# Turning the convolved input by DMA instead of on TensorE in a Mamba block: step sizes folded into exponents, eight places fewer in the bank ring, input norms split

## The reference

```python
x = input @ Wx.T; z = input @ Wz.T               # 512 wide
x = silu(causal_conv(x, conv_w, conv_b))         # 4 taps over time
b = x @ Wb.T; c = x @ Wc.T                       # 8 heads x 64 states
dt = softplus(x @ Wdt.T + b_dt)                  # one step size per token and head
# scan over time, per head:
state = exp(dt_t * a) * state + (dt_t * b_t) x_t ;  y_t = c_t . state
y = y + d_param * x                              # then norm per head, gate with silu(z), @ Wout.T
```

## Time and profile before

| | us |
|---|---|
| median of 3 runs | 1266.62 (1266.29 to 1266.91) |
| the profiled execution | 1265.6 |
| its span, first to last instruction | 1263.9 |
| PE busy in it | 1218.3 (96%) |
| DVE busy | 997.3 (79%) |
| ACT busy | 878.6 (70%) |
| POOL busy | 465.5 (37%) |

### The profile page before, as it was taken

How to read it: one execution, slowest core, us unless ns; L and a number is a source line. 1 busy time by engine, 2 the same in 40 slices (tenths; PEclk the granted TensorE clock), 3 DMA queues, 4 the chain that set the end, 5 groups by cost and what they waited for, 6 DMA issues and landing times.

```text
span 1263.9 us, 27616 instructions
## 1 busy us (share of the span) xinstructions
PE 1218.3 (96%) x10306; PEld 765.1 (61%) x10306; DVE 997.3 (79%) x2385; ACT 878.6 (70%) x1554; POOL 465.5 (37%) x557
## 2 busy tenths in 40 slices
PE   7999999999999999999999999999999999999896
PEld 5665657565565756656566565756656575564674
DVE  6666877788787796978779787778878789787687
ACT  6675677667776687766966678667787668776365
POOL 2131236142451524416343243623336152441332
PEclk9999999999999999999999999999999999999999
DMA  8011101111020110202111020111112111020001
GB/s 239 1 35 36 34 17 35 43 42 36 18 68 17 35 34 18 68 18 53 26 41 35 18 68 18 35 38 26 55 17 52 34 18 34 18 68 17 2 1 51
DMA packets 91829, 48.09 MB, mean 38 GB/s; under 512 B 63120, under 2 KB 89892, under 8 KB 91696
## 3 DMA queue, kind: packets, MB, share of 16 engines
q1 hardware_dynamic: 91696, 46.33, 14.9%
HBM read 22.72 MB, written 8.39 MB: 25 GB/s over the span
## 4 chain that ended last, share of the span: by engine, by line
PE 76%; DVE 14%; issue 5%; ACT 2%; POOL 2%; DVEq 0%; ACTq 0%; POOLq 0%
PE bank L1728 34%; PE bank L1945 8%; PE bank L1928 8%; PE bank L1837 5%; PE bank L1815 4%; PE bank L1899 3%; DVE xs L1303 3%; PE bank L1905 3%; PE bank L1873 3%; PE bank L1807 2%; PE bank L1860 2%; PE bank L1851 2%; DVE gn_stats L1442 2%; DVE yT L1481 1%; PE bank L1826 1%
## 5 line engine op out<-in xcount | busy, mean ns | idle before, releaser
L937 POOL TENSOR_TENSOR Cd<-Cd,CT 128x512 f32<-128x512 f32 x64 | 93.8, 1465 | 359.8 <-ACT Cd L1180 359.4
L1728 PE MATMUL bank<-sh,WbT 128*128 128x512 f16 x768 | 171.5, 379 | 1.9 <-DVE sh L1308 1.2
L1728 PE MATMUL bank<-sh,WcT 128*128 128x512 f16 x768 | 171.3, 379 | 0.0
L1208 ACT ACTIVATE hf<-bank,vectors,alpha 128x512 f32<-128x512 f32 x128 | 99.0, 776 | 52.0 <-PE bank L1928 30.2
L1303 DVE SCALAR_TENSOR_TENSOR xs<-xi,vectors,xs 128x512 f32<-128x512 f32 x168 | 125.1, 749 | 9.4 <-ACT xs L1085 5.7
L1728 PEld LDWEIGHTS bank<-sh,WcT 128*128 128x128 f16 x768 | 75.2, 98 | 86.6
L1728 PEld LDWEIGHTS bank<-sh,WbT 128*128 128x128 f16 x768 | 72.9, 98 | 87.1 <-DVE sh L1308 6.1
L1928 PE MATMUL bank<-uh,sign1T 128*128 128x512 f16 x512 | 121.6, 380 | 1.8 <-issue 1.7
L1945 PE MATMUL bank<-sign2T,hh 128*128 128x256 f16 x1024 | 117.2, 273 | 1.2 <-DVE hh L1543 1.1
L1945 PEld LDWEIGHTS bank<-sign2T,hh 128*128 128x128 f16 x1024 | 97.8, 98 | 21.7 <-ACT hf L1208 6.5
L868 POOL TENSOR_TENSOR rstd_mid<-var_eps_mid,power 128x4 f32<-128x4 f32 x16 | 16.2, 1011 | 227.3 <-DVE var_eps_mid L1258 227.3
(11 more groups left out here) (235 smaller groups left out, 2600.1 us busy)
## 6 DMA issues: line engine op xcount, KB each, us to landing
xt<-L_attn_input_tensor_dram SPq DMA_DIRECT2D x17, 512.0 KB, 4.1
u<-L_attn_input_tensor_dram SPq DMA_DIRECT2D x15, 512.0 KB, 3.9
out_dram<-u SPq DMA_DIRECT2D x15, 512.0 KB, 3.0
yT<-in_L_ffn_w_dram SPq DMA_DIRECT2D x2, 512.0 KB, 8.8
u<-in_L_ffn_w_dram SPq DMA_DIRECT2D x2, 512.0 KB, 9.3
BT<-in_L_attn_Wx_dram SPq DMA_DIRECT2D x1, 512.0 KB, 5.1
BT<-in_L_attn_Wz_dram SPq DMA_DIRECT2D x1, 512.0 KB, 4.5
zs<-in_L_attn_Wb_dram SPq DMA_DIRECT2D x1, 512.0 KB, 6.2
```

Of the source, the lines that this page charges most:

```text
L937: pool.tensor_tensor(Cd[n % 2][:, :, :], Cd[n % 2][:, :, :], CT[:, :, q * P:(q + 1) * P], ALU.mult)\
L1208: nc.scalar.activation(hf[f % 2][:, :], bank(t, ("H", j, f))[:, :], ACT.Gelu, bias=b1_col[:, f:f + 1], scale=alpha1[:, f:f + 1]).then_inc( ...
L1728: mm = nc.tensor.matmul(bank(t, key)[:, :], w[i][:, k, cols(m)], v[h][:, k, :], start=(a == 0), stop=(a == len(terms) - 1))
```

## The change

X leaves PE. SP issues, per chunk, two DMA transposes, one of each fp16 part of the convolved input, from `sh_rows`, whose layout is now tokens in runs of 128 per chunk (`[P, NQ, KI, P]`), into `x_turned`, which lies in chunks 3 and 0 of the tile `xi` (two buffers, for odd and even chunks). DVE adds the two parts into `xdt`, which now is 256 times the input, without the step size. The step size goes into the exponents: DVE floors it (`dt_floor`), ACT takes the logarithm of a 256th of it (`log_dt`), DVE spreads its negative over a wide tile (`log_wide`), and PE adds it with one more product each into `cums` and `sums`. The projections write and read through a view by chunk.

The bank ring has no X, so 107 places per element. The step `in_norm` is split: the high passes (`in_high`) stay in place, the four full passes come after `front` 2, and `xT` moves from before `front` 2 to between `carry` 1 and `back` 1; `end_tiles` moves behind `back` 1. In a first block ACT's `fold` of the tail comes before `gelu_table`, and `gelu_table` follows the new `ln_dt`. Some small tiles share memory (`abs_v` with `exp_v`, `e_rest` with `e_back`, `dt_floor` with `dt_raw`, `log_dt` with `log_u`), with waits for it.

```diff
@@ -192,10 +193,10 @@
-        steps += own(("log", j))
-        steps += tail(("mid_norm", j)) + own(("B", j, 1), ("decay", j)) + tail(("gelu_table",))
+        steps += own(("X", j, 0), ("X", j, 1), ("log", j))
+        steps += tail(("mid_norm", j)) + own(("B", j, 1), ("decay", j)) + tail(*[("fold", 1, m) for m in range(2 if j == 0 else 0)])
...
-        steps += tail(*[("fold", 1, m) for m in range(2 if j == 0 else 0)], ("ff_stat", j))
+        steps += own(("ln_dt", j)) + tail(("gelu_table",), ("ff_stat", j)) + own(("ln_wide", j))
@@ -218,20 +219,20 @@
 
-        norm, xT = [(who, "in_norm", nj)], [(who, "xT", nj), (who, "load", nj)]
+        norm, xT = [(who, "in_high", nj)], [(who, "xT", nj), (who, "load", nj)]
         steps += own(("decays", j), ("ends", j, 0), ("front", j, 0)) + ([(who, "in_mean", nj)] if first else []) + out[0]
...
             steps += weights(("alpha2", 0))
-        steps += own(("score", j, 1), ("carry", j, 0)) + norm + (own(("head_stat", 0, 0)) if j else [])
-        steps += out[1] + own(("back", j, 0)) + xT
+        steps += own(("X", j, 2), ("score", j, 1), ("X", j, 3), ("carry", j, 0)) + norm + (own(("head_stat", 0, 0)) if j else [])
+        steps += out[1] + own(("back", j, 0))
         def end(*keys):
...
 
-        steps += own(("E", j, 2), ("ends", j, 2), ("seg", j, 2), ("front", j, 2), ("score", j, 2)) + end(("end_tiles", j))
-        steps += own(("carry", j, 1), ("back", j, 1), ("E", j, 3), ("ends", j, 3), ("seg", j, 3), ("front", j, 3))
+        steps += own(("E", j, 2), ("ends", j, 2), ("seg", j, 2), ("front", j, 2)) + [(who, "in_norm", nj)]
+        steps += own(("score", j, 2), ("carry", j, 1)) + xT + own(("back", j, 1)) + end(("end_tiles", j)) + own(("E", j, 3), ("ends", j, 3), ("seg", j, 3), ("front", j, 3))
         steps += end(("end_mean", j)) + (end(("end_root", j)) if j else []) + own(("score", j, 3))
@@ -330,10 +331,12 @@
+        x_turned = [xi[:, KI - 1 if r else 0, 0:BLK].bitcast(F16).rearrange("p (i c f) -> p i c f", i=2, c=KI) for r in range(2)]
...
-        sh = [sb(f"sh{i}", [P, KI, BLK], F16) for i in range(2)]
+        sh_rows = [sb(f"sh{i}", [P, NQ, KI, P], F16) for i in range(2)]
+        sh = [v[:, :, :, :].rearrange("p q c t -> p c q t") for v in sh_rows]
@@ -342,12 +345,14 @@
-        v_dt, abs_v, exp_v, one_e, e_back, e_rest, log_u = (small(n) for n in (
-            "v_dt", "abs_v", "exp_v", "one_e", "e_back", "e_rest", "log_u"))
+        v_dt, exp_v, one_e, e_back, log_u = (small(n) for n in ("v_dt", "exp_v", "one_e", "e_back", "log_u"))
+        abs_v, e_rest = exp_v, e_back
...
+        dt_floor, log_dt = dt_raw, log_u
+        log_wide = sb("log_wide", [P, HP, PARTS, NQ * KI])
@@ -424,7 +429,7 @@
-                return [*[("seg", *at, g) for g in range(HP)], ("X", *at), ("Bt", *at)]
+                return [*[("seg", *at, g) for g in range(HP)], ("Bt", *at)]
@@ -511,6 +516,10 @@
+        x_rows = [Signal(sem(f"x_rows{r}"), NCH // 2, step=32) for r in range(2)]
+        ln_in = Signal(sem("ln_in"), NJ)
+        ln_out = Signal(sem("ln_out"), NJ)
+        ln_wide = Signal(sem("ln_wide"), NJ * HP)
@@ -810,6 +825,18 @@
+            def turn_tokens(t, j, q):
+                n = ch(j, q)
+                r = q % 2
+                s, sj, sq = two_before(t, n)
+                if q == 0:
+                    sp.wait_ge(*conv_out.count(t, (j + 1) * KI * (TAPS - 1)))
+                    sp.wait_ge(*sh_hi.count(t, (j + 1) * KI))
+                    sp.wait_ge(*sh_lo.count(t, (j + 1) * KI))
+                sp.wait_ge(*xdt_out.count(s, ch(sj, sq) + 1))
+                for i in range(2):
+                    sp.dma_start_transpose(x_turned[r][:, i, :, :], sh_rows[i][:, q, :, :].rearrange("p c t -> p (c t)")).then_inc(x_rows[r].sem, 16)
@@ -1022,14 +1050,16 @@
-            def input_norm(t, j):
-                if opening(t) and j == 0:
-                    return
+            def input_high(t, j):
...
+            def input_norm(t, j):
+                if opening(t) and j == 0:
+                    return
@@ -1056,7 +1086,6 @@
-                act.wait_ge(*full(s, ("X", sj, NQ - 1)))
@@ -1066,6 +1095,7 @@
+                    act.wait_ge(*xdt_out.count(s, (sj + 1) * NQ))
@@ -1117,15 +1147,24 @@
-                nc.scalar.activation(sh[0][:, c, :], xs[:, c, :], ACT.Copy, scale=SX).then_inc(sh_hi.sem, 1)
+                    for landed in x_rows:
+                        act.wait_ge(*landed.count(s, (sj + 1) * NQ // 2))
+                nc.scalar.activation(sh[0][:, c], by_chunk(xs[:, c, :]), ACT.Copy, scale=SX).then_inc(sh_hi.sem, 1)
...
+                p, pj = before_block(t, j)
+                act.wait_ge(*full(p, ("sums", pj)))
+                act.wait_ge(*ln_wide.count(p, (pj + 1) * HP))
...
+            def step_size_log(t, j):
+                act.wait_ge(*ln_in.count(t, j + 1))
+                nc.scalar.activation(log_dt[:, :, :], dt_floor[:, :, :], ACT.Ln, scale=1.0 / SX).then_inc(ln_out.sem, 1)
@@ -1337,7 +1380,9 @@
+                p, pj = before_block(t, j)
...
+                dve.wait_ge(*ln_out.count(p, pj + 1))
@@ -1348,14 +1393,25 @@
-                p, pj = before_block(t, j)
...
+                nc.vector.tensor_scalar(dt_floor[:, :, :], dt_t[:, :, :], DT_FLOOR, None, ALU.max).then_inc(ln_in.sem, 1)
...
+            def step_wide(t, j):
+                p, pj = before_block(t, j)
+                dve.wait_ge(*full(p, ("cums", pj)))
+                dve.wait_ge(*ln_out.count(t, j + 1))
+                raw = log_dt[:, :, :].rearrange("p q h -> p (q h)")
+                for g in range(HP):
+                    v = of_side(raw, g)[:, None].to_broadcast([P, PARTS // 2, NQ * KI // 2, 2])
+                    nc.vector.tensor_scalar(log_wide[:, g, PARTS // 2:PARTS, :].rearrange("p m (n f) -> p m n f", f=2), v, -1.0, None,
+                                            ALU.mult).then_inc(ln_wide.sem, 1)
@@ -1404,11 +1460,11 @@
-                for need in latest(full(t, ("X", j, q)), full(s, ("Y", sj, sq, HP - 1))):
-                    dve.wait_ge(*need)
+                dve.wait_ge(*full(s, ("Y", sj, sq, HP - 1)))
...
-                nc.vector.tensor_tensor(xdt[r][:, :, :], heads(bank(t, ("X", j, q))[:, :]), per_head(dt_t[:, q, :]),
-                                        ALU.mult).then_inc(xdt_out.sem, 1)
+                dve.wait_ge(*x_rows[q % 2].count(t, n // 2 + 1))
+                hi, lo = [x_turned[q % 2][:, i, :, :].rearrange("p c f -> p (c f)") for i in range(2)]
+                nc.vector.tensor_tensor(xdt[r][:, :, :], heads(hi), heads(lo), ALU.add).then_inc(xdt_out.sem, 1)
@@ -1725,7 +1781,7 @@
-                    mm = nc.tensor.matmul(bank(t, key)[:, :], w[i][:, k, cols(m)], v[h][:, k, :], start=(a == 0),
+                    mm = nc.tensor.matmul(by_chunk(bank(t, key)[:, :]), w[i][:, k, cols(m)], v[h][:, k], start=(a == 0),
@@ -1782,13 +1838,19 @@
-                                 start=True, stop=True).then_inc(full_sem(t, key), 1)
+                                 start=True, stop=False)
+                pe.wait_ge(*ln_wide.count(t, (j + 1) * HP))
+                nc.tensor.matmul(bank(t, key)[:, 0:P], log_wide[:, :, :, :].rearrange("p g a n -> p (g a n)"), ident[:, :],
+                                 start=False, stop=True).then_inc(full_sem(t, key), 1)
...
-                nc.tensor.matmul(bank(t, key)[:, 0:NQ * HEADS], after[:, :], da[:, :], start=True, stop=True)
+                nc.tensor.matmul(bank(t, key)[:, 0:NQ * HEADS], after[:, :], da[:, :], start=True, stop=False)
+                pe.wait_ge(*ln_out.count(t, j + 1))
+                nc.tensor.matmul(bank(t, key)[:, 0:NQ * HEADS], ident[:, :], log_dt[:, :, :].rearrange("p q h -> p (q h)"),
+                                 start=False, stop=True)
@@ -1807,13 +1869,12 @@
-                for name, src in (("X", xs), ("Bt", BT)):
-                    key = (name, j, q)
-                    for need in latest(empty(t, key), B_out.count(t, (j + 1) * KI), C_out.count(t, (j + 1) * KI)):
-                        pe.wait_ge(*need)
-                    for c in range(KI):
-                        mm = nc.tensor.transpose(bank(t, key)[:, cols(c)], src[:, c, cols(q)], ident[:, :])
-                    mm.then_inc(full_sem(t, key), 1)
+                key = ("Bt", j, q)
+                for need in latest(empty(t, key), B_out.count(t, (j + 1) * KI), C_out.count(t, (j + 1) * KI)):
+                    pe.wait_ge(*need)
+                for c in range(KI):
+                    mm = nc.tensor.transpose(bank(t, key)[:, cols(c)], BT[:, c, cols(q)], ident[:, :])
+                mm.then_inc(full_sem(t, key), 1)
```

35 lines of the change are left out of this document (22 added, 13 removed).

## The result

The changed kernel takes 1278.55 us (median of 4 runs, 1277.94 to 1279.25) where the kernel before takes 1266.57 (4 runs beside it): ratio 1.0095, 95% interval 1.0077 to 1.0112. It is 12.0 us slower. The forecast was 5.9 slower: the sign was right and 1278.55 lies in the wide range of 1254 to 1284, just above the 1269 to 1278 given to the forecast itself, but only half of the loss was foreseen. The profiled execution took 1277.94, its span is 1276.2.

A forecast was written before the change was run, and what follows sets the result against it. PE works 96% of the span, but waits on DVE and the DMA were taken to limit the gain. 5.6 + 4.2 - 3.5 + 2.1 - 2.5 = +5.9 on 1265.6 gives 1271.5, as median 1272.5 us; range 1254 to 1284.

The forecast's parts named there:

- the sign: Whole kernel: the change was forecast to make it slower, by 5.9 us, with a 60% chance given to slower.
- Added products: PE, every block: two more products for the exponents, 0.46 us a block, +5.6 us in all (bounds 3.6 and 9.9).
- the wait of H for uT: PE in block A, an element's second half: an idle of 0.22 us before H hides added products in 8 blocks.
- Block B: First half of the next element: DVE's state comes sooner, so the next block starts 0.5 us earlier, x7: -3.5.
- The string under the waits in A: Second half of an element: xT starts near 582.9, xi at 587.3, so 0.2 us is gained of 2.1.
- The waits themselves: PE in block A: stalls of 1.1 us before B's turn of chunk 3 and 1.2 us before xi.
- the contention of `xdt` with GpSimd: DVE's xdt reads two SBUF tensors beside GpSimd work: 0.15 us per chunk stage, 14 times, +2.1 (bounds 0 and 0.5 each).
- the landing: DMA of xT's low half in block A: taken to land 3.1 us after xT ends, at 587.3.
- The ring: Element border: with 107 places xi(0,1) waits for DVE's back of chunk 3, +0.6 us at 7 borders, +4.2.
- First and last block: Blocks with no tail or no next: X off PE saves some of its time, -2.5 us in all (bounds 0, -4).
- The deeper premise: PE, 64 chunks: X's transposes take some 0.5 us each chunk, so 31 us is the most that can be won.
- Rival 1: PE is the bound all along and the waits are not met: -31 + 5.6, 1241 us; 6% chance.

The follow-up runs named there:

- experiment 12: Changed kernel with xdt made from the high half of the turned X alone, one SBUF input instead of two: 1272.29 us, ratio 1.0048 to the kernel before.
- experiment 2: Changed kernel with three empty places in the bank ring, 110 per element: 1271.86 us, ratio 1.0050 to the kernel before.
- experiment 8: Changed kernel with three empty ring places and the next element's first xi product one step later, behind chunk 2's carried work: 1263.89 us, ratio 0.9981 to the kernel before.
- experiments 1: Changed kernel with xT and the input norms back in their old places, X still off PE: 1275.33 us, ratio 1.0070 to the kernel before.
- experiment 3: Changed kernel with xT and the norms in their old places and three empty ring places: 1271.11 us, ratio 1.0039 to the kernel before.
- Experiment 5: Kernel before with one of the four transposes of each X turn on PE, the other three left out: 1258.29 us, ratio 0.9938 to the kernel before.
- experiment 7: Kernel before with only the move of norms, xT and end sums, X still on PE: 1284.34 us, ratio 1.0136 to the kernel before.

## Why the prediction had the sign right and only half the size

- **Added products: right, with some luck.** 5.6 was forecast for 16 blocks; 5.5 is measured in 15 and 0.45 in the first. Thirteen of the 16 cost 0.40 to 0.45, three A blocks 0.04 to 0.16. So the wait of H for uT hides them in three A blocks, not in eight, and there it hides more than the 0.22.
- **Block B: right in mechanism and size.** YI of chunk 3 was put at 667.05 and stands at 667.04; -0.5 each was forecast, -0.6 measured. DVE's string is the one that was counted forward: 0.72 of waiting for GpSimd's state (0.6 forecast), and the state of chunk 3 at 666.5 in the frame (666.6). The agreement to 0.01 is chance.
- **The string under the waits in A: the step that failed.** The waits themselves were named rightly, 1.1 and 1.2 forecast, 1.08 and 1.09 measured, but the string that sets them was priced too low in two terms. The first is the contention of `xdt` with GpSimd, taken at 0.15 a chunk stage "as most of it falls in waits". In A it doesn't: it goes through `Cd`, `xdw` and `state` on GpSimd into `carry` 1, `xT` and the transfer, and is worth 0.5 or more (experiment 12). `xT` was put at 582.9 and stands at 583.5, xi at 587.3 and is at 587.9. In B it does fall in waits, as far as that run shows. The rule of the Trainium skill that the prediction cites (GPSIMD Engine Reference, the specifications table) agrees with these rows, but the sum needed a price. The second term is the landing, taken at 3.1 after the issue: two of seven took 4.3 and 4.4 (see the landings below).
- **The ring: right in mechanism, 0.6 forecast, 0.8 measured** per border (experiment 2), 1.3 us more in all. Together with the contention this is more than the 2.4 by which the typical A blocks miss; what gave the rest back I didn't trace.
- **Not in the sum at all: landings that vary.** A typical A costs 1.1, 0.35 over the 0.75 that the ring and the contention gave it, 2.4 in seven. Three of seven cost 2.2 to 2.4 and make another 3.6. In two of them the low half lands 4.3 and 4.4 us after its issue instead of 3.1; PE's rows:

```profile
898.64 1.46 PE L1784 MATMUL bank<-xh,WxT 128*128 128x512 f16 x6 [2.32 <-issue]
...
1051.98 1.46 PE L1784 MATMUL bank<-xh,WxT 128*128 128x512 f16 x6 [2.35 <-issue]
```

  In the third, block 1, a stretch at a lower granted clock (0.60) follows waits of 0.27 and 1.25; the columns of the windows are as above:

```profile
127.45 0.65 PE L1876 MATMUL bank<-ident,BT 128*128 128x128 f32 x4 [1.25 <-DVE yT L1491]
128.03 1.37 PE L1898 MATMUL bank<-CT,BT 64*128 64x128 f32 x16
129.33 1.12 PE L1912 MATMUL bank<-xdw,bt 128*64 128x64 f32 x16
...
130.00:132.80 2.80, 2.80 (x42) 2.22 (x38) 1.17 (x4) 0.70 (x2) 0.61 (x1) 0.60 0.00 0
```

  Experiment 2 has the same waits there (0.28 and 1.24), keeps its full clock, and its block 1 costs no more than a typical one, so the third block's price is the clock's. The 5.0 at the end of the earlier trace rows was there to be read. The kernel before had 1.2 to 3.0 us between the landing and xi, the changed one has none, so the median of the landings was the wrong figure for a sum. The 2.4 and the 3.6 are A's miss of 6.0 (11.2 measured, 5.25 forecast), and A's miss is about the forecast's.
- **First and last block:** -2.5 forecast, -0.2 in the changed kernel's profiled execution (with 0.45 of added products in it). Most of the miss is the clock in the last block. There PE waits 2.97 us for `Cd` in all kernels of this order, and what its clock does then differs. Windows of 15 us that begin just before that wait, of the changed kernel, experiment 2 and experiment 8 (columns as above), have a granted clock of 0.77, 0.89 and 1.00, and the stretch from the last `seg` of chunk 0 to the end is 0.3, 1.6 and 3.0 shorter than before:

```profile
1180.00:1195.00 15.00, 10.99 (x104) 7.90 (x103) 9.16 (x20) 8.80 (x15) 6.75 (x6) 0.77 0.19 36
```

```profile
1175.00:1190.00 15.00, 10.98 (x119) 7.72 (x119) 10.11 (x21) 9.40 (x16) 7.18 (x7) 0.89 0.20 37
```

```profile
1167.00:1182.00 15.00, 10.87 (x148) 7.69 (x150) 11.76 (x23) 9.26 (x17) 7.48 (x7) 1.00 0.18 37
```

  The kernel before has 0.89 in the same place, so experiment 2's -1.4 is the term at a like clock, -1.9 without the added products. B's better figure (1.6 with its share of the contention) and this worse one nearly cancel: luck.
- **The deeper premise** was that up to 31 us of X are there to be won, and that the moved steps decide how much. I held to it after the result as well (experiments 1 and 3). Experiment 5 shows about a third of it within reach in the old order. PE without gaps isn't the same as a PE that sets the time: close behind it came DVE, which in experiment 3 runs from `xT` to `carry` 1 without a pause. Rival 1, PE as the bound all along, falls with it.
- **Still open:** why single landings take 4.4 us or more. They do in the kernel before, and in experiment 7 with X on PE, so X's transfers aren't needed for it; no run varied what else is in flight. Nor does any run show what decides whether the half clock follows a wait of 1.2 to 3 us.

## What to carry to other kernels

Before taking work off the busiest engine, ask what the others do in the same microseconds: replace the work by nothing for one run (as in experiment 5) and see how much of it comes off. When a step moves to where its consumer waits for its transfer, count with the long end of that transfer. Follow every engine in the string, also the one that looks idle enough: here GpSimd's queue set when the step could start. And look for independent work on the consumer's engine to put in between; here that one step was worth 8 us. When places leave a round of buffers, check which reader each first use of the next round falls behind.
